# The filling of a 32-step software pipeline: forward transform first, row spreading between two mixes, first coefficients weighed first

## The reference

```
x = x + conv_block(layernorm_over_channels(x))
t = tokens(x);  t = t + ffn(layernorm(t));  x = image(t)

conv_block(x):
    x[:, :12] = conv3x3(x[:, :12])              # 12 of the 48 channels
    x = conv1x1(x, w_in)                        # 48 -> 254
    xf = rfft2(8x8 patches of x) * fft_w        # one weight per channel and frequency
    a, b = split(irfft2(xf))                    # 127 + 127
    return conv1x1(gelu(a) * b, w_out)          # 127 -> 48
ffn(t): y = q(relu(q(t @ W1 + b1)) @ W2 + b2)   # 48 -> 192 -> 48, operands rounded to fp8 e5m2
```

## Time and profile before

| | us |
|---|---|
| median of three runs | 700.97 |
| span of the profiled execution (first to last instruction) | 699.4 |
| PE busy in the span | 666.5 |
| DVE busy | 597.9 |
| ACT busy | 536.8 |
| POOL busy | 456.9 |

### The profile page before, as it was taken

The page is one execution under the profiler, slowest core; times in us unless marked ns, Lnnn a source line. Parts: engine busy times, 40 slices in busy tenths (PEclk is TensorE's granted clock), DMA queues, the critical chain, the costliest instruction groups (busy, mean ns, idle before and its releaser), DMA issues.

```text
span 699.4 us, 19176 instructions
## 1 busy us (share of the span) xinstructions
PE 666.5 (95%) x6620; PEld 529.3 (76%) x6620; DVE 597.9 (85%) x1159; ACT 536.8 (77%) x1087; POOL 456.9 (65%) x347
## 2 busy tenths in 40 slices
PE   4879999999999999999999999999999999999984
PEld 4657877778778877787878877787788777887751
DVE  7637889988988899988988899889888999877877
ACT  4244568888888888888889888888888888877784
POOL 2605677767777777677776877677777876753353
PEclk9989999999999999999999999999999999999995
DMA  4434445444544554445444544545445543342102
GB/s 102 79 78 118 121 113 131 112 126 128 142 120 118 142 140 121 114 120 138 127 123 131 139 131 107 132 121 144 121 116 144 139 129 103 100 119 87 47 23 68
DMA packets 52207, 80.73 MB, mean 115 GB/s; under 512 B 20823, under 2 KB 36079, under 8 KB 52111
## 3 DMA queue, kind: packets, MB, share of 16 engines
q1 hardware_dynamic: 50031, 78.56, 43.2%
q10 hardware_dynamic: 2080, 0.94, 0.6%
HBM read 63.17 MB, written 16.30 MB: 114 GB/s over the span
## 4 chain that ended last, share of the span: by engine, by line
PE 87%; DVE 3%; DMA 3%; issue 2%; ACT 1%; SPq 1%; POOL 1%; DVEq 0%; ACTq 0%; POOLq 0%
PE inva L532 17%; PE invb L539 15%; PE mixp L519 13%; PE misc L548 8%; PE misc L803 8%; PE misc L619 4%; PE misc L519 4%; PE misc L663 3%; PE misc L784 3%; PE misc L568 2%; PE misc L577 2%; PE misc L653 2%; PE mixp L632 2%; PE mixp L639 2%; DMA xin<-in_x_dram 1%
## 5 line engine op out<-in xcount | busy, mean ns | idle before, releaser
L1555 POOL TENSOR_TENSOR st<-st,neg_half 128x16 f32<-128x16 f32 x32 | 93.3, 2915 | 129.2 <-DVE st L1459 129.2
L532 PEld LDWEIGHTS inva<-inv,gmix 128*127 128x127 f32 x1024 | 123.4, 191 | 25.3 <-issue 16.6
L532 PE MATMUL inva<-inv,gmix 128*127 128x128 f32 x1024 | 141.0, 281 | 0.6 <-DVE gmix L1234 0.6
L1234 DVE TENSOR_TENSOR gmix<-mixp,freq_w 128x508 f32<-128x508 f32 x192 | 122.6, 680 | 16.9 <-PE mixp L519 16.9
L539 PE MATMUL invb<-inv,gmix 128*127 128x128 f32 x1024 | 134.7, 274 | 0.1
L539 PEld LDWEIGHTS invb<-inv,gmix 128*127 128x127 f32 x1024 | 126.2, 191 | 2.1 <-DVE hbuf L1245 0.5
L897 ACT ACTIVATE hid<-misc 128x512 f16<-128x512 f32 x180 | 94.1, 599 | 17.7 <-PE misc L619 17.7
L1245 DVE TENSOR_TENSOR hbuf<-gact,invb 127x512 f32<-127x512 f32 x128 | 87.4, 683 | 22.2 <-ACT gact L889 17.7
L1584 POOL TENSOR_TENSOR st<-st,neg_half 128x16 f32<-128x16 f32 x31 | 95.4, 3077 | 16.4 <-DVE st L1313 15.9
L906 ACT ACTIVATE hid<-hid 128x512 fp8e5<-128x512 f16 x174 | 93.2, 619 | 0.0
L889 ACT ACTIVATE gact<-inva 127x512 f32<-127x512 f32 x128 | 77.5, 605 | 19.9 <-PE inva L532 19.3
(11 more groups left out here) (184 smaller groups left out, 1358.2 us busy)
## 6 DMA issues: line engine op xcount, KB each, us to landing
taps<-cz_scratch SPq DMA_DIRECT2D x63, 292.2 KB
xin<-in_x_dram SPq DMA_DIRECT2D x64, 192.0 KB, 3.3
xres<-in_x_dram SPq DMA_DIRECT2D x64, 192.0 KB, 4.1
out_dram<-ob SPq DMA_DIRECT2D x60, 192.0 KB, 2.6
taps<-cz_scratch SPq DMA_DIRECT2D x63, 146.1 KB
crm<-rm_scratch SPq DMA_DIRECT2D x58, 96.0 KB
cx<-in_x_dram SPq DMA_DIRECT2D x32, 96.0 KB
cz_scratch<-cz SPq DMA_DIRECT2D x63, 48.8 KB
```

Source lines behind the costliest of these rows:

```text
L532: mm = pe.matmul(inva[0:HID, q * PX:(q + 1) * PX], gmix[:, s % 2, q, 0:HID], inv[:], start=True, stop=True, skip_group_check=True)
L1234: dve.tensor_tensor(gmix[:, s % 2, 2 * q:2 * q + 2, 0:HID2], pair[q][:, 0:2 * HID2].rearrange("p (e c) -> p e c", e=2), freq_w[:], ALU.mul ...
L1555: pool.tensor_tensor(st1[:, 6, :], st1[:, 5, :], neg_half[:], ALU.pow).then_inc(pow1, 1)
```

## The change

It reorders steps 2 and 3 and moves two PSUM banks; no arithmetic changes.

- ACT, step 2: `order_x` of band 3 goes from ahead of `convs` to behind `zpix`.
- PE, step 3: the forward transform of band 0 goes ahead of turning band 3 (its second half now goes to bank 2, not bank 0); `keep_busy(6)` goes; `spread(2)` goes from the end of step 2 to between mix 0 and mix 1; the rows of band 3 go from inside inverse 1 to the end of the step (into bank 2).
- ACT, step 3: the two `zh` copies go ahead of the copies of band 3; `rm_t` goes to the end.
- DVE, step 3: the new function `first_coefficients` holds the order: weigh 0, `early_channels(2)`, weigh 1, gate 0, weigh 2, the sum of band 3, gate 1, its squares, weigh 3, gate 2, rows.

```diff
@@ rows_bank, coefficient_bank
+        def coefficient_bank(t, q):
+            return bank[3] if q == 0 else bank[2 if t == (0, 3) else 0]
+        def rows_bank(a):
+            return mixp[0] if a >= ROWS_EARLY else bank[2 if a == 3 else 3]
@@ PE step
-                    pe.wait_ge(rmT_ready, upto(before(0) if t[1] > 3 else 0))
+                    pe.wait_ge(rmT_ready, upto(before(0) if t[1] > 3 else 2 if t[1] == 3 else 0))
...
+                if live(t, 0) and t[1] != 3:
+                    turn_x(t)
                 if live(t, 3):
+                    forward(t)
+                if t[1] == 3:
+                    turn_x(t)
                 if live(t, 4):
                     inverse(t, 4, 3)
-                if peeled and a == 3:
-                    pe.wait_ge(rmT_ready, 3)
-                    keep_busy(6)
                 if live(t, 3):
                     if peeled and a == 3:
                         pe.wait_ge(set_act, 10)
                     mix(t, 0)
                     pe.wait_ge(lo_ready, upto(2 * n + 2, 2 * STEPS))
+                    if peeled and a == 3:
+                        spread(2)
                     pe.wait_ge(xsq_ready, upto(2 * a + 2, 2 * STEPS))
                     mix(t, 1)
...
-                    if live(t, 0) and 3 <= a < ROWS_EARLY:
+                    if live(t, 0) and 3 < a < ROWS_EARLY:
                         rows(t, 0)
...
                 if live(t, 2):
                     convolve(t)
-                    if peeled and a == 2:
-                        spread(2)
                 if live(t, 3):
                     inverse(t, 3, 2)
+                if a == 3:
+                    rows(t, 0)
@@ ACT step
-                if live(t, -1):
+                if live(t, -1) and a != 2:
                     order_x(t, -1)
...
                     act.activation(dst, src, ACT.Copy, scale=1.0 / SCALE).then_inc(conv_read, 1)
+                if a == 2:
+                    order_x(t, -1)
                 if live(t, 3):
                     gelu(t, 3, 2)
+                if a == 3:
+                    rows(t, 0)
@@ DVE
+            def first_coefficients(t):
+                dve.wait_ge(set_act, 10)
+                weigh(t, 0)
+                early_channels(2)
+                weigh(t, 1)
+                gate(t, 3, 0)
+                weigh(t, 2)
+                sums(t)
+                means(t)
+                gate(t, 3, 1)
+                squares(t)
+                weigh(t, 3)
+                gate(t, 3, 2)
+                rows(t, 0)
```

More of the change, by code:

```diff
@@ L666, in turn_rest, with turn_x, forward @@
                         mm.then_inc(tT_done, 1)
+            def turn_x(t):
+                a, l = at(t, 0), at(t, 6)
+                peeled = not FIRST <= t[1] < LAST
+                if not peeled:
+                    pe.wait_ge(hid16_ready, upto(6 * l + 5))
+                if a == 0:
+                    pe.wait_ge(eye_in, 16)
+                pe.wait_ge(xord_ready, upto(a + 1))
+                for i in range(PAIRS):
+                    mm = pe.transpose(bank[i // 4][:, (i % 4) * 128:(i % 4) * 128 + XSPAN],
+                                      xord[:, i * PX:(i + 1) * PX], eye[0:XSPAN, 0:XSPAN])
+                    if i % 4 == 3:
+                        mm.then_inc(xT_done, 1)
+                if a == 1:
+                    keep_busy(12)
+                    spread(0)
+                if a == 2:
+                    spread(1)
+                    setup()
+            def forward(t):
+                a, n = at(t, 0), at(t, 3)
+                if FIRST <= t[1] < LAST:
+                    pe.wait_ge(rmT_ready, upto(a))
+                pe.wait_ge(conv_read, upto(n + 1))
+                pe.wait_ge(zpix_ready, upto(n + 1))
+                for i in range(PAIRS):
+                    if i == 4 and n > 0:
+                        pe.wait_ge(xsq_ready, upto(2 * a + 1, 2 * STEPS))
+                    mm = pe.matmul(coefficient_bank(t, i // 4)[0:KSPAN, (i % 4) * PX:(i % 4 + 1) * PX],
+                                   zpix[:, ring(t, 3), i, 0:KSPAN], fwd[:], start=True, stop=True,
+                                   skip_group_check=True)
+                    if i % 4 == 3:
+                        mm.then_inc(coef_done, 1)
             def drain():
@@ L912, in rows @@
                 act.wait_ge(rm_out, upto(64 * (a - 3)))
[L913 removed]
+                act.activation(rm_t[:], rows_bank(a)[0:32, 0:128], ACT.Copy).then_inc(rmT_ready, 1)
             def layers():
@@ L1060, in step @@
                 filling = isinstance(t[0], int) and t[1] < 3
[L1061 to L1071, removed]
+                if live(t, 0) and a != 3:
+                    pixels(t)
                 if filling and t[1] == 2:
@@ L1438, in step @@
                     low_parts(t, 1)
+                if a == 3:
+                    first_coefficients(t)
+                    return
                 if live(t, 0):
[L1440 to L1445, removed]
+                    means(t)
                 if live(t, 4):
@@ L1464, in step @@
                     setup()
-                if live(t, 3) and not first_mix:
+                if live(t, 3):
                     weigh(t, 0)
-                if live(t, 3):
                     weigh(t, 1)
```

96 lines of the change are left out of this document (46 added, 50 removed).

## The result

The changed kernel takes 714.5 us (median of 5 runs, 712.44 to 716.5), the kernel before 700.94 us (5 runs, 700.03 to 700.98): ratio 1.0203, 95% interval 1.0186 to 1.0221. It is 2% slower. The direction and the mechanism were forecast, the size not in full: 710.0 was forecast, with a range up to 713.5. The profiled execution took 716.18 us, among the longer of the five, so its span differs from the span before by more than the medians do.

What follows compares the result with a forecast made beforehand. Bounds: the filling's late `convs` and the chain from band 3's rows to band 2's taps. `stream` of band 2 5.5 late, plus 2.0 and 2.0 us of low clock, less 0.5: 9.0, giving 710.0 us, range 705.5 to 713.5 (its own 707.5 to 712.5).

Steps and rivals of the forecast that it cites:

- forward transform starts: PE, band 0: with `order_x` of band 3 behind `zpix`, the transform can start at 39.7 us.
- channels of band 2 ready: DVE: spreading behind mix 0 leaves these channels ready at 46.9 to 47.0 us, against 47.07 before.
- from there to `stream` of band 1: SP's queue of store, wait and four loads stays the same; taps land at 57.3 us.
- `stream` of band 1 starts: PE arrives by 52.8 us, waits at least 4.5 for taps landing at 57.3; 1.2 us of gain left.
- from there to SP's `rows_out` of band 3: 4.8 us to the end of gate 2, 1.06 to SP's take-up, 2.0 of low clock behind PE's wait.
- from there to `stream` of band 2: Rows to taps of band 2: 19.7 us of DRAM trips, POOL work and DMA issue, plus 0.1, unchanged.
- lateness added behind it: Behind `stream` of band 2: 2.0 us for the second low clock, less 0.5 for covered small PE waits.
- the taps of band 1, therefore, land when they did: DMA of band 1's taps: same queue behind unmoved channels of band 2, landing taken as 57.3 us.
- the first rival: Filling runs at low clock: forward transform and turning take 1.7 us more, everything behind shifts; 711.7 us, chance 0.25.
- not slower: Rival: taps of band 1 land before about 52 us, loss nearly all repaid; 700 to 702 us, chance 0.07.
- the clock holds: Rival: clock holds or returns at once in PE's waits, only the chain counts; 706.0 us, chance 0.13.
- the 58.6: Latest landing of band 1's taps by the skill's rule: traffic end 56.6 plus 2.0 us; set aside for 57.6 at most.

Runs made afterwards that it cites:

- e1_clock: Changed kernel with 32 and 20 identity matmuls filling PE's waits ahead of `stream` of bands 1 and 2: 712.86 us, ratio 1.0166.
- e2_rows: Changed kernel with the rows of band 3 ahead of `stream` of band 1 again on PE, DVE and ACT: 704.41 us, ratio 1.0050.
- e5_fill_clock: Changed kernel with `keep_busy(26, bank[1])` for `keep_busy(16, bank[1])` ahead of `stream` of band 0: 713.69 us, ratio 1.0174.
- e3_channels: Changed kernel with spreading and channels of band 2 back in step 2, rows still at the end of step 3: 706.25 us, ratio 1.0077.
- w1: Changed kernel with early spreading and channels of band 2, and rows of band 3 behind inverse 1 on PE: 700.44 us, ratio 0.9984.
- w3: Kernel before with `order_x` of band 3 behind `zpix` and DVE's squares of band 3 ahead of weigh 0: 698.19 us, ratio 0.9974.
- w4: Kernel before with late `order_x`, squares of band 3 ahead of weigh 0, and `spread(2)` ahead of `stream` of band 0: 699.11 us, ratio 0.9980.
- after_again: Changed kernel run once more, unaltered, against the kernel before: 715.57 us, ratio 1.0220.
- e6_rows_alone: Kernel before with only the rows of band 3 moved to the end of step 3 on PE, ACT and DVE: 709.1 us, ratio 1.0124.
- e7_spread_alone: Kernel before with only the spreading of band 2 between mix 0 and mix 1, its channels behind weigh 0: 707.55 us, ratio 1.0108.
- w2: Kernel before with `order_x` of band 3 behind `zpix` and `spread(2)` ahead of `stream` of band 0: 699.2 us, ratio of eleven executions 0.9977.
- e4_order_x: Kernel before with only ACT's `order_x` of band 3 moved behind `zpix` of band 0: 698.64 us, ratio 0.9971.

## Why the prediction was right and wrong

Right: that it is slower, by which mechanism, and through which instructions. The trace after has each of the steps in its order, and from `stream` of band 1 on with its size. Against the profiled execution (span 714.4, 15.0 us more), step by step:

| step | forecast | measured |
|---|---|---|
| forward transform starts | 39.7 | 40.63 |
| channels of band 2 ready | 46.9 to 47.0 | 49.59 |
| from there to `stream` of band 1 | 10.3 | 12.9 |
| `stream` of band 1 starts | 57.3 | 62.48 |
| from there to SP's `rows_out` of band 3 | 4.8 + 1.06 + 2.0 = 7.9 | 8.0 |
| from there to `stream` of band 2 | 19.8 | 19.8 |
| lateness added behind it | 2.0 - 0.5 | 15.0 - 12.8 = 2.2 |

The step that failed is "the taps of band 1, therefore, land when they did": the term of the sum that was mis-sized is the start of `stream` of band 1, 57.3 forecast and 62.5 measured. I booked 1.2 us of gain there; it was 4.0 us of loss, and the other terms carried it on unchanged. Two things made it, about half each.

*The filling at the low clock*, 2.6 us. This was the first rival, at a chance of 0.25 and with 711.7 us; its condition came true, and the time was longer still by what follows. The forward transform took 3.56 us instead of 1.94, and `convolve` 1.06 instead of 0.66. Of the profiles of kernels with the changed filling (the changed kernel twice, e1_clock, e2_rows, e5_fill_clock, e3_channels) the transform ran low in all but e3_channels, in which the spreading takes up PE's wait ahead of `stream` of band 0 down to 0.85 us; w1, with that same spreading but 2.24 us of idleness behind it, fell again. The idleness alone does not decide it: w3 idled 2.46 us there and kept the full clock, w4 idled 2.47 and lost it. I gave the low clock too small a chance though the trace of before had it in the same place, and had no better reason for the full clock than that the idleness was shorter.

*The way from the channels to the taps*, 2.6 us, is three pieces. From the stores' issue to the first load SP took 5.09 us for 3.32 (1.8 more), which came and went from run to run. The last load took 5.26 us from its issue (57.22) to `stream` (62.48), where I had 4.1 (1.2 more). The four issues between took 0.3 less (the three sum to 2.6 before rounding). In after_again, the same kernel, the last load took 4.56 us, and with the 4.85 us of its stores `stream` of band 1 started at 61.97.

I took 57.3 for the end of the last load in the kernel before, and its own trace bears that out. In the five profiles in which PE waited for these taps with nothing else on the queues (the changed kernel twice, e1_clock, e5_fill_clock, e6_rows_alone), `stream` started 0.6 to 1.1 us behind the last traffic: here traffic ends at 61.8 and `stream` starts at 62.48. In the kernel before the traffic ends by 56.6, so these taps were there at 57.2 to 57.7, an estimate from these rows. The mistake was to carry this one execution's duration over as a constant: its last load moved its bytes within 3.4 us of the issue, those five needed 3.7 to 4.6. In the eight profiles in which PE waited for the taps of band 1 (those five, e2_rows, e7_spread_alone and w3), the last load took 4.56 to 5.26 us from issue to `stream`, so 57.3 was the early end, and a range for this term was missing.

The Trainium skill (DMA: Bandwidth & Descriptors, on the anatomy of one DMA) puts about 2 us of fixed cost on a DMA, most of it behind the last byte, in a section on DMAs issued from GpSimd; SP issues these. The traces here do not show 2 us at this place but the 0.6 to 1.1 us above, so the 58.6 reckoned from it lies nearer to the measured start only by chance.

The rival "not slower" did not come true for the change, and its condition was then made true in e3_channels: with the taps early, the rows' place alone still gave 706.25, not 700 to 702. The rival "the clock holds" gave 706.0 against 712.86 in e1_clock, which had the two waits filled but not the filling; it too fails by the way from the channels to the taps and by the low filling.

Put into the kernel before one at a time, the two costly parts come near the whole: the rows alone cost 9.0 us (709.1 to 700.1) and the spreading alone 7.5; with ACT's winning order (about -2) the sum is 14.5, and the change has 13.6. Taken out of the changed kernel one at a time they overlap: undoing the rows gives 10.1, undoing the spreading 8.3, together 18.4, and undoing both 14.1 (w1). These are differences of medians from several chips, on which the kernel before took 700.06 to 700.94 us. The forward transform and the first coefficients ahead of the rest were not run alone; w1 against w2 shows neither gain nor loss from them.

## What to carry to other kernels

In a software pipeline's filling, find for each engine the piece of its work on which a long way through DRAM hangs (here a 2 us spreading and a 0.3 us transpose, with 13 and 20 us of stores, loads and small operations behind them), and do not place it behind the work that you are bringing forward before you have followed that way to its end. That mixes start 5 us sooner gains nothing if the next wait ends with a DMA whose start did not move. And where a wait is not seen in the trace because data came in time, its landing time stands in no row: bound it by the end of its traffic, and give the term a range from several executions before booking a gain against it.

## What the runs showed of the hardware

- In the filling the granted clock fell from 1.00 to 0.50 behind idle stretches of PE of 1.4 to 4.2 us between short pieces of work, but not each time. The same 16 passes of the forward transform took 1.94 us (w3) and 3.75 us (w1, e5_fill_clock). With 2.46 us of idleness ahead of `stream` of band 0 the clock held in w3, with 2.47 it fell in w4. Adding 10 filler matmuls and so leaving 1.40 us of idleness instead of 2.20 did not keep it up in e5_fill_clock; in e3_channels, with 0.85 us, it held. What decides is open.
- The same two stores of 48.8 KB, issued at 42 us or later, let SP go on after 3.2 to 3.4 us in the profiles of seven kernels (before, e2_rows, e4_order_x, e5_fill_clock, e6_rows_alone, e7_spread_alone, w3) and after 4.9 to 5.1 us in three profiles (the changed kernel twice, e1_clock). Issued at 38 us, right behind SP's other loads, they took 4.6 to 5.1 us (e3_channels, w1, w4).
- The last load of the taps of band 1 let `stream` start 4.56 to 5.26 us behind its issue in eight profiles, and 0.6 to 1.1 us behind the end of the traffic in the five of them with nothing else on the queues.
- Executions of the changed kernel lie within 4.1 us (712.44 to 716.5), and again in after_again (714.19 to 718.29); in both the ones with a mean granted clock of 0.970 are the longest. Those of the kernel before lay within 1.0 us in the first 5 and within 3.7 us (699.12 to 702.77) in 23 on the chip of after_again.
- One of w2's 12 executions took 1341.22 us. It was the one profiled, so w2 has no other trace. In it the second matmuls of the inverse transform took 451 ns in the mean, not 274, and PE was busy for 1317.2 us, not 666.5, with the same number of instructions, while DVE's operations took what they always do. TensorE worked at about half its speed throughout; the granted clock in the trace reads 1.00 all the same.

```profile
L539 PE MATMUL invb<-inv,gmix 128*127 128x128 f32 x1024 | 263.9, 451 | 0.0
```
